# Two-layer graph network on one core: four small operands of VectorE in the second edge pass kept in PSUM in place of SBUF

## The chip, the cores and the metric

The kernel runs on one core of a Trainium2 chip. The metric is the device time of one execution in microseconds (us); the number compared is the median of several executions. Durations of single instructions are in nanoseconds (ns) where marked so. The engines are TensorE (PE; its weight loads are listed as PEld), VectorE (DVE), ScalarE (ACT), GpSimd (POOL) and SyncE (SP).

## The reference, cut to what matters

There are 3125 nodes with 128 features, and 100000 edges (src, dst), sorted by dst in the inputs. Two graph layers follow each other, each with a residual and a layer norm. The change is in the edge work of the second:

```python
def _L1_gnn_ref(X, edge_index, Wq, Wk, Wphi, Wy_w, Wy_b, We):
    src, dst = (edge_index[0], edge_index[1])
    q = (X @ Wq)[src]
    k = (X @ Wk)[dst]
    e = jnp.tanh(q + k)
    scores = e @ Wphi
    scores = scores - jnp.max(scores)
    exp_scores = jnp.exp(scores)
    denom = jax.ops.segment_sum(exp_scores, src, num_segments=N)
    alpha = exp_scores / (denom[src] + 1e-09)
    vy = (X @ Wy_w + Wy_b)[dst]
    ve = e @ We
    msg = alpha[:, None] * (vy + ve)
    out = jax.ops.segment_sum(msg, src, num_segments=N)
    return out
```

## The kernel before, in words

**Stages.** The kernel sorts the edges by src, runs the first layer's edge network and its first edge pass, then the node work between the layers, the second edge pass, and a last node stage. On the profiled execution the second edge pass starts at 1646 us and its last step ends near 2698 us.

**Tiles.** Edges are handled in 196 groups of 512: 128 partitions by 4 (GT). Nodes are handled in 25 blocks of 128 (BN). A step pairs one group with one block that occurs in it. As the edges are sorted by block, there are 220 steps (STEPS, 196 + 25 - 1): mostly a new group, now and then the same group again with the next block. The steps' groups and blocks were worked out on the chip and stand in a plan that the engines read as they go.

**The gathers.** GpSimd does nothing in this pass but fetch the rows of dst (192 numbers, key and value). For every group it issues 4 indirect DMAs (L1575), one for each of the 4 columns, 784 in all. Each takes its 128 row numbers from `rec_all` in SBUF and puts rows of `kv_table` (in DRAM) into one of 8 places (RING1) of `landed_rows`. Before the fourth of a group it waits until the group before has landed, and tells ScalarE (`ready`). From the ninth group on it waits before a group until the step that last used the place is done.

**A step.** All engines keep step through semaphores, each with its instructions in a fixed order, working up to four steps ahead. ScalarE moves the group's landed rows to `row_v` (L1661; tile sum_acc in the profile). VectorE makes `seg_rel`, the node's place in the block (L1723), and the one-hot of it (`hot`, L1726: iota row compared with seg_rel, 128x512, bf16). TensorE transposes the one-hot (L1603), ScalarE copies it (L1690), TensorE takes the queries with it (L1616), VectorE adds them to the keys (`add_queries`, L1740), ScalarE takes tanh (L1671). VectorE multiplies by the attention vector (`score`, L1756, 128x256), sums (L1759), and adds the penalty of edges outside the block and takes the lane's maximum (L1762). ScalarE squares the distance to the block's middle (L1675), VectorE makes the penalty of it (`outside`, L1733). The maximum over the lanes goes through TensorE (L1623), VectorE (`highest`, L1748) and TensorE (L1627) to ScalarE, which makes the exponentials (L1683, 4 a partition) and the factor for the older sums (L1685). VectorE spreads the exponentials over the one-hot (`spread_p`, L1769, 128x512), TensorE forms the messages (L1633), VectorE adds them to the block's sums (`take`, L1780, 128x193).

**What sets the order.** VectorE's order in a step is add_queries two ahead, outside three ahead, hot four ahead, highest one ahead, score two ahead, spread_p one ahead, take. ScalarE's is the row move three ahead, tanh two ahead, the square four ahead, exponentials one ahead, then the copies of query rows (L1667) and transposed one-hot four ahead. Sems `cleared` (GpSimd's three fills) and `cleared_v` (VectorE's fills) hold all three engines back at the start.

**Memory.** The iota row (`iota_n`, 128 columns), attention vector (`phi_b`, 64), penalties (`pen`, 5 steps by 4) and exponentials (`p_e`, 2 by 4) are in SBUF. Of the eight PSUM banks the pass uses 0 to 5; L1740, L1748 and L1780 have one input in PSUM. The instructions that the change touches have both tensor inputs in SBUF:

```python
v.tensor_tensor(onehot_v[...], iota_n..., seg_rel..., ALU.is_equal)     # L1726
v.tensor_tensor(prod[...], row_v[...], phi_b..., ALU.mult)              # L1756
v.tensor_tensor_reduce(sc[...], raw[...], pen[...], ...)                # L1762
v.tensor_tensor(probT_v[...], onehot_v[...], p_e..., ALU.mult)          # L1769
```

Of the kernel before, what the change touches and what calls it, by code (L numbers as in the profile page):

```python
# [5 lines left out]
ALU = mybir.AluOpType  # L6
# [8 lines left out]
AD = 64  # L15
BN = 128
# [5 lines left out]
GT = 4  # L22
# [22 lines left out]
RING = 5  # L45
# [42 lines left out]
def build(nc, i, out):  # L88
    with ExitStack() as ctx:
        def sb(name, shape, dt=F32):  # L90
            return ctx.enter_context(nc.sbuf_tensor(name, shape, dt))
# [21 lines left out]
        iota_n = sb("iota_n", [128, BN])  # L113
# [26 lines left out]
        phi_b = sb("phi_b", [128, AD])  # L140
# [13 lines left out]
        bank = [turn_bank[:, :]] + [twin[n // 2][:, n % 2 * 512:(n % 2 + 1) * 512] for n in range(4)]  # L154
# [3 lines left out]
        def step_of(s, k, ahead=0, unroll=SU):  # L158

            return s + (k + ahead) // unroll, (k + ahead) % unroll  # L160
# [5 lines left out]
        def is_first(n, slots=1):  # L166

            return isinstance(n, int) and n < slots

        def inside(edge, k, ahead, unroll=SU):  # L170


            if edge == "start":
                return k + ahead >= unroll
            return edge is None or k + ahead < edge

        def rounds(eng, body, before, total=STEPS, unroll=SU):

            for k in range(unroll - before, unroll):
                body(-1, k, "start")  # L180
            first = 0
            if total == NB:
                for k in range(unroll):
                    body(0, k, None)
                first = 1
            turns = -(-total // unroll) - 1
            left = total - turns * unroll
            with eng.Fori(first, turns) as s:
                for k in range(unroll):
                    body(s, k, None)  # L190
            for k in range(left):
                body(turns, k, left)
# [796 lines left out]
        with ExitStack() as c2:  # L989
# [14 lines left out]
            onehot_v = onehot[:, :, :].rearrange("p u (j n) -> p u j n", j=GT)  # L1004
# [41 lines left out]
            def within(value, top):  # L1046
                return nc.s_assert_within(value, 0, top, skip_runtime_bounds_check_because="the plan is cut to these bounds")
# [453 lines left out]
        with ExitStack() as c4:  # L1501
            def sb4(name, shape, dt=F32):
                return c4.enter_context(nc.sbuf_tensor(name, shape, dt))

            def sem4(name):
                return c4.enter_context(nc.semaphore(name))
# [12 lines left out]
            onehot_v = onehot[:, :, :].rearrange("p u (j n) -> p u j n", j=GT)  # L1519
# [2 lines left out]
            hotT = sb4("hotT", [BN, 2, GE], BF16)  # L1522
            off = sb4("off_window", [128, 2, GT])
            middle = sb4("middle", [128, 1])
            pen = sb4("pen", [128, RING, GT])
            prod = sb4("prod", [128, GT, AD])
            raw = sb4("raw_score", [128, GT])
            sc = sb4("sc", [128, 2, GT])
# [3 lines left out]
            top_row = sb4("top_row", [1, 128])  # L1532
            top = sb4("top_run", [1, SU])
            neg_top = sb4("neg_top_run", [128, SU])
            p_e = sb4("p_e", [128, 2, GT])

            cleared = sem4("cleared1")
            cleared_v = sem4("cleared1v")
# [9 lines left out]
            prod_done = sem4("prod_done1")  # L1548
# [11 lines left out]
            with nc.Block() as block:  # L1560
# [30 lines left out]
                @block.tensor  # L1591
                def _(pe):
                    pe.sem_inc(stepped, SU)
                    pe.wait_ge(cleared, 3)
                    pe.wait_ge(cleared_v, 5)

                    def turn(s, k):
                        n = s * SU + k
                        if not is_first(n):
                            pe.wait_ge(hotT_done, n)  # L1600
                        pe.wait_ge(hot_done, n + 1)
                        for j in range(GT):
                            last = pe.transpose(bank[1][0:BN, :].bitcast(BF16)[:, j * 128:(j + 1) * 128],  # L1603
                                                onehot_v[:, k % RING, j, :], identb[:, :])
                        last.then_inc(hotT_ps, 1)

                    def queries(s, k):

                        n = s * SU + k
                        pe.wait_ge(q_in, n + 1)  # L1610
                        pe.wait_ge(hotT_done, n + 1)
                        if not is_first(n):
                            pe.wait_ge(sum_done, n)
                        for j in range(GT):
                            for part in range(3):
                                last = pe.matmul(bank[0][:, j * AD:(j + 1) * AD], hotT[:, k % 2, j * 128:(j + 1) * 128],  # L1616
                                                 qb[:, k % RINGQ, part * AD:(part + 1) * AD], start=(part == 0), stop=(part == 2))
                        last.then_inc(query_ps, 1)

                    def turn_max(s, k):  # L1620
                        pe.wait_ge(score_done, s * SU + k + 1)
                        pe.sem_inc(ticks, 1)
                        pe.transpose(bank[2][0:1, 0:128], lane_max[:, k % 2:k % 2 + 1], identf[:, :]).then_inc(maxT_ps, 1)  # L1623

                    def share_top(s, k):
                        pe.wait_ge(top_done, s * SU + k + 1)
                        pe.matmul(bank[3][:, 0:1], ones[0:1, :], top[0:1, k:k + 1], start=True, stop=True).then_inc(top_ps, 1)  # L1627

                    def messages(s, k):
                        pe.wait_ge(spread, s * SU + k + 1)  # L1630
                        pe.wait_ge(summed, s * SU + k + 1)
                        for j in range(GT):
                            last = pe.matmul(bank[4 + k % 2][0:BN, 0:KV + 1], probT_v[:, k % 2, j, :], row_v[:, k % RING, j, AD:RK],  # L1633
                                             start=(j == 0), stop=(j == GT - 1))
                        last.then_inc(stepped, 1)

                    def body(s, k, edge):
                        if inside(edge, k, 1):
                            share_top(*step_of(s, k, 1))
                        if inside(edge, k, 3):  # L1640
                            queries(*step_of(s, k, 3))
                        if inside(edge, k, 4):
                            turn(*step_of(s, k, 4))
                        if inside(edge, k, 2):
                            turn_max(*step_of(s, k, 2))
                        if inside(edge, k, 1):
                            messages(*step_of(s, k, 1))
                    rounds(pe, body, 4)

                @block.scalar  # L1650
                def _(act):
                    act.wait_ge(cleared, 3)
                    act.wait_ge(cleared_v, 5)

                    def move_rows(s, k, at):
                        n = s * SU + k
# [52 lines left out]
                def _(v):  # L1709
# [3 lines left out]
                    v.memset(nil[:, :], 0.0).then_inc(cleared_v, 1)  # L1713
                    v.memset(top[:, :], NONE).then_inc(cleared_v, 1)
                    v.memset(neg_top[:, :], -NONE).then_inc(cleared_v, 1)
                    v.wait_ge(cleared, 3)
                    v.wait_ge(cleared_v, 5)

                    def hot(s, k, g):

                        n = s * SU + k
                        group = rec_all[:, bass.ds(within(g, GROUPS - 1), 1), :].rearrange("p o (j w) -> p (o j) w", w=W2)
                        v.tensor_scalar(seg_rel[:, k % 2, :], group[:, :, 0], base1[:, bass.ds(n, 1)], None,  # L1723
                                        ALU.subtract).then_inc(placed, 1)
                        v.wait_ge(placed, n + 1)
                        v.tensor_tensor(onehot_v[:, k % RING, :, :], iota_n[:, :].unsqueeze(1).to_broadcast([128, GT, BN]),  # L1726
                                        seg_rel[:, k % 2, :].unsqueeze(2).to_broadcast([128, GT, BN]),
                                        ALU.is_equal).then_inc(hot_done, 1)

# [22 lines left out]
                    def score(s, k):  # L1752

                        n = s * SU + k
                        v.wait_ge(tanh_done, n + 1)
                        v.tensor_tensor(prod[:, :, :], row_v[:, k % RING, :, KV:KV + AD],  # L1756
                                        phi_b[:, :].unsqueeze(1).to_broadcast([128, GT, AD]), ALU.mult).then_inc(prod_done, 1)
                        v.wait_ge(prod_done, n + 1)
                        v.tensor_reduce(raw[:, :], prod[:, :, :], AX.X, ALU.add).then_inc(raw_done, 1)  # L1759
                        v.wait_ge(raw_done, n + 1)  # L1760
                        v.sem_inc(ticks, 1)
                        v.tensor_tensor_reduce(sc[:, k % 2, :], raw[:, :], pen[:, k % RING, :], 1.0, floor[:, 0:1],  # L1762
                                               ALU.add, ALU.max, lane_max[:, k % 2:k % 2 + 1]).then_inc(score_done, 1)
# [194 lines left out]
```

## Time and profile before

| | |
|---|---|
| median of 3 runs | 2787.11 us (2782.03 to 2795.92) |
| the profiled execution, its own time | 2772.86 us |
| its span, first to last instruction | 2771.2 us |
| mean granted TensorE clock in it | 0.898 of full |
| TensorE / weight loads busy | 78% / 52% of the span |
| VectorE, ScalarE, GpSimd busy | 66%, 55%, 61% |

The profile is of one execution. "Busy" counts the time in which an engine has an instruction under way; "idle before" is the time an engine stood still just ahead of a group of instructions, with what ended it ("issue": nothing that the profile shows). A line with a q behind the engine's name is its sequencer. The shares are a mean over stages with different limits. The profiled execution took 14.3 us less than the median of the runs.

### The profile page before, as it was taken

What the parts mean: (1) busy time and instruction counts of PE and PEld (TensorE: products, weight loads), DVE (VectorE), ACT (ScalarE), POOL (GpSimd) and SP (SyncE); (2) the same over time, 40 slices, a digit from 0 to 9 for tenths busy, and PEclk for the clock granted to TensorE, in tenths of its full rate; (3) what the DMA queues carried; (4) which work ended last, traced back from release to release, by engine and by line L of the source; (5) the groups of instructions that cost most, each with busy time, mean ns of one, the idle gap of its engine ahead of it and who ended that gap; (6) DMA issues with size and microseconds to landing.
All of it is one profiled execution on the core that took longest, in us unless ns stands there. A gap on an engine that the chain in (4) does not pass through costs nothing. (4 is left out here: it accounts for less than half of the span.)

```text
span 2771.2 us, 64649 instructions
## 1 busy us (share of the span) xinstructions
PE 2167.7 (78%) x16604; PEld 1454.2 (52%) x16604; DVE 1815.4 (66%) x6215; ACT 1528.7 (55%) x4445; POOL 1687.2 (61%) x1772
## 2 busy tenths in 40 slices
PE   6799999996888888888888376776777777777773
PEld 4333333334666666666667345555555555555552
DVE  8965464105666666766666637777778777777764
ACT  2466766774555555555554115555555555555541
POOL 1377777765555565556552017777777777777750
PEclk9999999997999999999999658889888889888985
DMA  9244444544444444444443012222222222222220
GB/s 97 72 137 130 134 134 145 143 114 133 152 153 154 156 149 150 155 149 151 156 149 104 5 43 76 74 75 74 74 76 77 75 73 74 77 77 75 76 53 24
DMA packets 211670, 290.63 MB, mean 105 GB/s; under 512 B 87104, under 2 KB 136149, under 8 KB 211568
## 3 DMA queue, kind: packets, MB, share of 16 engines
q0 software_dynamic: 76160, 172.95, 23.0%
q1 hardware_dynamic: 135408, 116.54, 14.1%
q8 instruction: 38, 0.62, 0.1%
q14 instruction: 64, 0.52, 0.1%
HBM read 183.24 MB, written 28.70 MB: 76 GB/s over the span
## 5 line engine op out<-in xcount | busy, mean ns | idle before, releaser
L1575 POOL DMA_INDIRECT sum_acc<-kv_table,rec_all x784 | 790.0, 1008 | 239.2 <-issue 229.9
L1079 POOL DMA_INDIRECT area_b<-h_table,src_g x448 | 454.6, 1015 | 339.9 <-issue 184.7
L514 POOL DMA_INDIRECT early<-h_table,src_g x336 | 331.2, 986 | 222.0 <-ACT sum_acc L729 142.0
L729 ACT ACTIVATE sum_acc<-twin,bias 128x1024 f32<-128x1024 f32 x294 | 317.9, 1117 | 155.1 <-PE twin L599 151.3
L1661 ACT COPY sum_acc<-sum_acc 128x768 f32 x220 | 183.4, 834 | 378.0 <-POOLq L1581 290.4
L1176 ACT COPY y_sb<-bank 128x512 f32<-128x512 f32 x293 | 171.5, 585 | 329.4 <-PE bank L1140 327.7
L1149 PE MATMUL bank<-hs,y_sb 128*128 128x129 f32 x2344 | 323.6, 282 | 0.7 <-ACT y_sb L1172 0.6
L599 PE MATMUL twin<-area_b,wc 64*128 64x512 f32 x1176 | 313.5, 634 | 10.9 <-ACT sum_acc L729 10.9
L1140 PE MATMUL bank<-identf,hs 128*128 128x128 f32 x1172 | 196.2, 292 | 138.9 <-DMA hs<-area_b 137.2
L1149 PEld LDWEIGHTS bank<-hs,y_sb 128*128 128x128 f32 x2344 | 296.8, 198 | 5.1 <-issue 3.8
L1267 DVE SCALAR_TENSOR_TENSOR sum_acc<-sum_acc,shrink,bank 128x129 f32 x293 | 102.2, 349 | 277.0 <-ACT m_old L1193 172.6
L1633 PE MATMUL bank<-sum_acc,probT 128*128 128x193 f32 x880 | 222.5, 408 | 27.0 <-DVE probT L1769 24.6
L1140 PEld LDWEIGHTS bank<-identf,hs 128*128 128x128 f32 x1172 | 128.5, 146 | 205.9 <-issue 205.9
L1633 PE MATMUL twin<-sum_acc,probT 128*128 128x193 f32 x880 | 214.3, 397 | 26.9 <-DVE probT L1769 24.9
L1633 PEld LDWEIGHTS bank<-sum_acc,probT 128*128 128x128 f32 x880 | 181.7, 234 | 53.1 <-DVE probT L1769 52.1
L1633 PEld LDWEIGHTS twin<-sum_acc,probT 128*128 128x128 f32 x880 | 174.5, 226 | 52.9 <-DVE probT L1769 51.5
L1756 DVE TENSOR_TENSOR prod<-sum_acc,phi_b 128x256 f32<-128x256 f32 x220 | 93.7, 426 | 152.8 <-ACT sum_acc L1671 151.5
L1623 PE MATMUL twin<-identf,lane_max 128*1 128x128 f32 x220 | 63.1, 287 | 163.8 <-DVE lane_max L1762 163.7
L599 PEld LDWEIGHTS twin<-area_b,wc 64*128 64x128 f32 x1176 | 95.7, 186 | 155.7 <-issue 78.9
L1769 DVE TENSOR_TENSOR probT<-onehot,p_e 128x512 f32<-128x512 bf16 x220 | 152.0, 691 | 11.9 <-ACT p_e L1683 11.8
L1726 DVE TENSOR_TENSOR onehot<-iota_n,seg_rel 128x512 bf16<-128x512 f32 x220 | 153.4, 697 | 7.6
L1235 DVE TENSOR_TENSOR y_sb<-onehot,w_g 128x384 f32<-128x384 bf16 x293 | 157.1, 536 | 0.0
(311 smaller groups left out, 4540.1 us busy)
## 6 DMA issues: line engine op xcount, KB each, us to landing
hs<-area_b SPq DMA_DIRECT2D x293, 258.0 KB, 2.4
area_b<-in_edge_attr SPq DMA_DIRECT2D x97, 256.0 KB, 2.9
rows_table<-early POOLq DMA_DIRECT2D x84, 258.0 KB, 3.0
area_b<-rows_table POOLq DMA_DIRECT2D x84, 258.0 KB
sum_acc<-kv_table,rec_all POOLq DMA_INDIRECT x784
area_b<-h_table,src_g POOLq DMA_INDIRECT x448
early<-h_table,src_g POOLq DMA_INDIRECT x336
kv_table<-sum_acc SPq DMA_DIRECT2D x25, 96.0 KB, 1.6
```

The costliest lines, as they stand in the source:

```text
L514: pool.indirect_dma_start(out=early[:, g % RINGE, j, 0:D], out_offset=None, in_=h_table, in_offset=bass.IndirectOffsetOnAxis(ap=src_g[:, e ...
L599: pe.matmul(twin[p % 2][:, half * GE:(half + 1) * GE], wc[half * DE:(half + 1) * DE, m * D:(m + 1) * D], eaT[half * DE:(half + 1) * DE, o ...
L729: act.activation(hid_words[:, first:first + 2 * GE], twin[p % 2][:, :], ACT.Relu, bias=bias1[:, m:m + 1]).then_inc(hid_sb, 1)
L1079: pool.indirect_dma_start(out=landed_rows[:, k * GT + j, 0:D], out_offset=None, in_=h_table, in_offset=bass.IndirectOffsetOnAxis(ap=src_g[ ...
L1140: last = pe.transpose(bank[0][:, j * 128:(j + 1) * 128], hs[:, k % SH, j, 0:D], identf[:, :])
L1149: last = pe.matmul(bank[5 + k % 3][:, 0:D + 1], both[:, k % 4, j, :], hs[:, k % SH, j, :], start=(j == 0), stop=(j == GT - 1))
L1176: act.copy(hsT[:, k % 2, :], bank[0][:, :]).then_inc(hsT_done, 1)
L1235: v.tensor_tensor(both[:, k % 4, :, WN:].rearrange("p j (m n) -> p j m n", m=M), onehot_v[:, k % SH, :, :].unsqueeze(2).to_broadcast([128, ...
L1575: pool.indirect_dma_start(out=landed_rows[:, g % RING1 * GT + j, :], out_offset=None, in_=kv_table, in_offset=bass.IndirectOffsetOnAxis(ap ...
L1633: last = pe.matmul(bank[4 + k % 2][0:BN, 0:KV + 1], probT_v[:, k % 2, j, :], row_v[:, k % RING, j, AD:RK], start=(j == 0), stop=(j == GT - 1))
L1661: act.copy(row_v[:, k % RING, :, 0:KV], landed_rows[:, bass.ds(within(at, (RING1 - 1) * GT), GT), :]).then_inc(moved, 1)
L1726: v.tensor_tensor(onehot_v[:, k % RING, :, :], iota_n[:, :].unsqueeze(1).to_broadcast([128, GT, BN]), seg_rel[:, k % 2, :].unsqueeze(2).to ...
```

## The change

The iota row and the attention vector are copied once, at the start of the pass, to PSUM bank 6. The penalties are written by VectorE to bank 6, the exponentials by ScalarE to bank 7. The four instructions above read them there. `cleared_v` counts two more.

```diff
-            pen = sb4("pen", [128, RING, GT])
...
-            p_e = sb4("p_e", [128, 2, GT])
+            iota_ps = bank[6][:, 0:BN]
+            phi_ps = bank[6][:, BN:BN + AD]
+            pen = bank[6][:, 256:256 + RING * GT].rearrange("p (u j) -> p u j", u=RING)
+            p_e = bank[7][:, 0:2 * GT].rearrange("p (q j) -> p q j", q=2)
...
                     pe.wait_ge(cleared, 3)
-                    pe.wait_ge(cleared_v, 5)
+                    pe.wait_ge(cleared_v, 7)
...
                     act.wait_ge(cleared, 3)
-                    act.wait_ge(cleared_v, 5)
+                    act.wait_ge(cleared_v, 7)
...
                     v.memset(neg_top[:, :], -NONE).then_inc(cleared_v, 1)
+                    v.tensor_copy(iota_ps, iota_n[:, :]).then_inc(cleared_v, 1)
+                    v.tensor_copy(phi_ps, phi_b[:, :]).then_inc(cleared_v, 1)
                     v.wait_ge(cleared, 3)
-                    v.wait_ge(cleared_v, 5)
+                    v.wait_ge(cleared_v, 7)
...
-                        v.tensor_tensor(onehot_v[:, k % RING, :, :], iota_n[:, :].unsqueeze(1).to_broadcast([128, GT, BN]),
+                        v.tensor_tensor(onehot_v[:, k % RING, :, :], iota_ps.unsqueeze(1).to_broadcast([128, GT, BN]),
                                         seg_rel[:, k % 2, :].unsqueeze(2).to_broadcast([128, GT, BN]),
                                         ALU.is_equal).then_inc(hot_done, 1)
...
                         v.tensor_tensor(prod[:, :, :], row_v[:, k % RING, :, KV:KV + AD],
-                                        phi_b[:, :].unsqueeze(1).to_broadcast([128, GT, AD]), ALU.mult).then_inc(prod_done, 1)
+                                        phi_ps.unsqueeze(1).to_broadcast([128, GT, AD]), ALU.mult).then_inc(prod_done, 1)
```

L1733, L1762, L1683 and L1769 keep their text; their `pen` and `p_e` are now in PSUM.

## Rows read from the trace of the kernel before

**Rows 1.** The page, busy us (share of the span) and instructions

```profile
PE 2167.7 (78%) x16604; PEld 1454.2 (52%) x16604; DVE 1815.4 (66%) x6215; ACT 1528.7 (55%) x4445; POOL 1687.2 (61%) x1772
```

**Rows 2.** Busy time of each engine from 1651 to 2680 us

```profile
sum 1029.00, PE 736.14 PEld 577.57 DVE 788.54 ACT 594.72 POOL 789.93; mean PE 184.03 PEld 144.39 DVE 197.14 ACT 148.68 POOL 197.48
```

**Rows 3.** GpSimd's gathers: page group (busy, mean ns, idle); line (ns min/median/max), waits

```profile
L1575 POOL DMA_INDIRECT sum_acc<-kv_table,rec_all x784 | 790.0, 1008 | 239.2 <-issue 229.9
...
L1575 POOL DMA_INDIRECT sum_acc<-kv_table,rec_all x784: 940/946/1467, 1651.0 to 2679.1; - x196
...
  DMA sum_acc<-kv_table,rec_all: 6.4, 21
```

**Rows 4.** The page's groups, ScalarE's move of landed rows

```profile
L1661 ACT COPY sum_acc<-sum_acc 128x768 f32 x220 | 183.4, 834 | 378.0 <-POOLq L1581 290.4
```

**Rows 5.** Timeline (start, duration in us), VectorE's L1780 in two successive steps

```profile
2216.20 0.41 DVE L1780 SCALAR_TENSOR_TENSOR area_b<-area_b,shrink_,bank 128x193 f32 x1
...
2219.99 0.41 DVE L1780 SCALAR_TENSOR_TENSOR area_b<-area_b,shrink_,twin 128x193 f32 x1
```

**Rows 6.** Groups of GpSimd from 2200 to 2300 us

```profile
L1575 POOL DMA_INDIRECT sum_acc<-kv_table,rec_all x74 | 78.1, 1056 | 22.9 <-issue 21.6 <-DMA sum_acc<-kv_table,rec_all 0.9 <-PE twin L1633 0.3
```

**Rows 7.** Timeline, three of the 31 long gathers and VectorE's instruction beside each

```profile
2209.33 0.41 DVE L1756 TENSOR_TENSOR prod<-sum_acc,phi_b 128x256 f32<-128x256 f32 x1
2209.36 1.21 POOL L1575 DMA_INDIRECT sum_acc<-kv_table,rec_all  x1 [0.63 <-issue]
...
2234.13 0.69 DVE L1769 TENSOR_TENSOR probT<-onehot,p_e 128x512 f32<-128x512 bf16 x1
...
2234.46 1.18 POOL L1575 DMA_INDIRECT sum_acc<-kv_table,rec_all  x1 [0.30 <-issue]
...
2299.47 0.69 DVE L1726 TENSOR_TENSOR onehot<-iota_n,seg_rel 128x512 bf16<-128x512 f32 x1
...
2299.56 1.43 POOL L1575 DMA_INDIRECT sum_acc<-kv_table,rec_all  x1 [0.30 <-issue]
```

**Rows 8.** Timeline, gathers that begin while L1740 or L1780 runs

```profile
2273.95 0.42 DVE L1740 TENSOR_TENSOR sum_acc<-bank,sum_acc 128x256 f32<-128x256 f32 x1
2274.01 0.95 POOL L1575 DMA_INDIRECT sum_acc<-kv_table,rec_all  x1 [0.30 <-issue]
...
2302.47 0.41 DVE L1780 SCALAR_TENSOR_TENSOR area_b<-area_b,shrink_,bank 128x193 f32 x1
2302.54 0.95 POOL L1575 DMA_INDIRECT sum_acc<-kv_table,rec_all  x1 [0.30 <-issue]
```

**Rows 9.** Groups of VectorE and ScalarE by shape (busy us, mean ns)

```profile
L1726 DVE TENSOR_TENSOR onehot<-iota_n,seg_rel 128x512 bf16<-128x512 f32 x220 | 153.4, 697 | 7.6
L1769 DVE TENSOR_TENSOR probT<-onehot,p_e 128x512 f32<-128x512 bf16 x220 | 152.0, 691 | 11.9 <-ACT p_e L1683 11.8
L782 DVE TENSOR_TENSOR area_b<-area_b 128x512 f32<-128x512 f32 x146 | 100.0, 685 | 0.0
L1756 DVE TENSOR_TENSOR prod<-sum_acc,phi_b 128x256 f32<-128x256 f32 x220 | 93.7, 426 | 152.8 <-ACT sum_acc L1671 151.5 <-issue 0.4
L1740 DVE TENSOR_TENSOR sum_acc<-bank,sum_acc 128x256 f32<-128x256 f32 x220 | 93.4, 424 | 27.4 <-issue 13.9 <-ACT sum_acc L1661 5.0
...
L1733 DVE TENSOR_SCALAR pen<-off_window 128x4 f32<-128x4 f32 x220 | 36.5, 166 | 0.0
...
L782 DVE TENSOR_TENSOR area_b<-area_b,bank 128x512 f32<-128x512 f32 x7 | 4.8, 680 | 0.0
...
L1685 ACT ACTIVATE shrink_<-neg_top_run 128x1 f32<-128x1 f32 x220 | 61.3, 279 | 0.0
...
L1680 ACT ACTIVATE neg_top_run<-twin 128x1 f32<-128x1 f32 x220 | 35.7, 162 | 60.2 <-PE twin L1627 58.0
```

**Rows 10.** Timeline of the pass's start, GpSimd's large fill and VectorE's last

```profile
1646.69 4.11 POOL L1568 MEMSET area_b<- 128x4825 f32 x1
...
1647.01 0.07 DVE L1715 MEMSET neg_top_run<- 128x10 f32 x1
```

## Prediction

> **What bounds the kernel now.** The change touches one stage, the second edge pass, so I read in this order: the page's busy shares, the busy times of that stage, GpSimd's transfers, the waits, and last the timeline around single transfers. Over the whole span no engine is full [rows 1]. In the pass, from GpSimd's first row gather at 1651.0 us to the end of its last at 2680.05 us, a stretch of 1029 us, VectorE is busy 789 us and GpSimd 790 us [rows 2], a tie that tells nothing. The gaps decide. GpSimd's 784 gathers leave only 239.2 us idle in front of them, 0.305 us each; 229.9 us of that is GpSimd's own issue time, and the 21 gaps put down to a landed transfer average 6.4/21 = 0.305 us, no longer than the others [rows 3]. 790.0 + 239.2 = 1029.2 us: GpSimd goes from one gather to the next without a pause and is the whole stretch. The other side waits for it: ScalarE's move of the landed rows, once a step, waits 290.4 us in total for GpSimd [rows 4]. VectorE can do a step in 3.79 us when rows are there [rows 5], where a step now gets 1029/220 = 4.68 us. So the pass lasts as long as GpSimd's 784 gathers, and a VectorE instruction made faster or slower costs nothing by itself. What counts is what the change does to a gather.
>
> **What lengthens a gather.** A gather has a median of 946 ns, but a mean of 1008 and a maximum of 1467 [rows 3]. 784 x (1008 - 946) = 48.6 us is the excess. In the stretch from 2200 to 2300 us the mean is 1056 ns over 74 [rows 6]. I went through these 74 beside VectorE's timeline: 31 are over 960 ns, and each of the 31 began while L1726, L1769 or L1756 was running, and ended some 0.82 us after that instruction did. The first of them, one between, and the last: L1756 ends at 2209.74, the gather at 2210.57; L1769 at 2234.82, the gather at 2235.64; L1726 at 2300.16, the gather at 2300.99 [rows 7]. What these three have in common is two tensor inputs in SBUF. Where L1740 or L1780 runs across a gather's beginning the gather takes 0.95 us [rows 8]; these are as long, but one of their two tensors is in PSUM. So GpSimd, at the start of a gather, seems to need something that a VectorE instruction with two SBUF inputs holds until its end, and one with a single SBUF input leaves free. The change makes exactly these three (and the short L1762) instructions with one SBUF input.
>
> A page speaks against this reading. The Trainium skill, "SBUF — State Buffer", section "Who interferes with whom", infers that a two-input tensor operation takes only the read half of the ports VectorE shares with GpSimd, while descriptor generation needs the write half, so that such an operation would not stall it; by that there is nothing to gain. The timeline here shows such stalls, up to 1467 - 946 = 521 ns, so the sum goes by the rows.
>
> **The change part by part.**
> - L1726 (iota to PSUM), L1769 (exponentials to PSUM), L1756 (attention vector to PSUM): each loses its second SBUF input. GpSimd: all 784 gathers at 946 ns, so -48.6 us, all of it on the path. The order of operands differs (the PSUM one is first in L1726, second in the others); L1740 has it first, L1780 second, and neither stalls a gather [rows 8], so I take the whole.
> - The length of these instructions. Same operation, same 128x512 shape: L782 with both inputs in SBUF 685 ns, with one in PSUM 680; at 128x256, both in SBUF 426 (L1756), one in PSUM 424 (L1740) [rows 9]. So the price of a PSUM input is -5 to 0 ns, and I take 0. What no row shows is a PSUM operand read with repetition, as iota, vector and exponentials are here; the low end is 0, the high end, a read at half rate, is priced under the rivals.
> - The penalty (L1733) is written to PSUM and L1762 reads it there. No row has VectorE writing PSUM. L1733 takes 166 ns [rows 9]; I bound it by that much either way and take 0. It lies under GpSimd's pace; without that cover it is at most 220 x 0.17 = 37 us.
> - ScalarE writes the exponentials (L1683) to PSUM. No row has that either. The nearest pair is one-column work from PSUM, 162 ns (L1680), against one from SBUF, 279 ns (L1685) [rows 9]: a memory moved on the read side is worth 117 ns. Bounds +/-0.12 us a step, value 0; hidden by the same cover, at most 26 us if it is gone. ScalarE's row move (L1661) still waits behind GpSimd.
> - Two copies at the start, and a wait for 7 in place of 5 on three engines. 128 and 64 columns, by L1740's 424 ns for 256 under 0.8 us for both. VectorE is through its fills at 1647.1 us and then waits for GpSimd's 4.11 us fill, which ends at 1650.8 [rows 10]: 3.7 us of cover. TensorE and ScalarE wait for the same fill. Cost 0; at most 0.8 us if GpSimd's fill were gone. No DMA and no queue is moved, and GpSimd's program is unchanged.
>
> Sum: the stretch falls from 1029.2 to 784 x (0.946 + 0.305) = 980.8 us, -48.6 us (the three decimals round). The profiled execution goes from 2772.9 to about 2724 us. It was faster than all runs shown, whose median, 2787.1, is 14.3 us above it; I keep that distance and forecast 2738.5 us, 1.7% less. What is late next is still GpSimd, at 4 x 1.251 = 5.0 us a group; 220 steps over 196 groups then have 980.8/220 = 4.46 us each, against 3.79 in a free step. A landing will not be late: none delays a gather beyond the ordinary 0.305 us now [rows 3], and 3 gathers still lie between a group's last gather and the wait for it.
>
> **The rivals.**
> - A, slower: repeated reads from PSUM run at half rate. From 128x256 to 128x512 an SBUF instruction grows by (697 - 426)/256 = 1.06 ns an element [rows 9]; again as much for 512, 512 and 256 elements is +1.36 us a step, 3.79 + 1.36 = 5.15 us x 220 = 1133 us against 1029: +104 us, 2891 us. It decides as soon as the addition passes 4.68 - 3.79 = 0.89 us a step; from 0.67 us on it begins to eat the gain. For it: no row shows such a read. Against: all PSUM inputs in the rows run at SBUF's rate. The Trainium skill, "VectorE: DVE Perf Modes", section "The TRN2 errata", gives a VectorE access to PSUM 62 cycles more than to SBUF, an estimate of 65 ns each; the pairs above do not show it, and it would only move the point nearer. Chance 5%.
> - B, no change: GpSimd's stall is bound to VectorE's length or output, not to its second SBUF input, and stays. For it: L1726 and L1769 are the longest instructions and write the most. Against: L1756, as short as L1740, stalls too, and L1740 does not. This is also the outcome in which the change does not do what it says. 2787 us, chance 7%.
> - C, a part: L1726, which keeps its repeated SBUF operand beside PSUM, goes on stalling. Of the 74 x (1056 - 946) ns = 8.1 us excess in the stretch [rows 6], 5.1 us lie in the 15 gathers that L1726 held, the last gather of [rows 7] among them, so the gain is 48.6 x 3.0/8.1 = 18 us: 2769 us. Against it: L1740 has the same placing, PSUM first and SBUF second. Chance 8%.
>
> **How the numbers follow.** The forecast has 80%. Its own range: runs of before spread by -5 to +9 us about their median, and the excess, read from one execution, may be 40 to 60 us; 2722 to 2756 us. To hold 8 in 10 with the rivals I reach to C: 2722 to 2770. A measurement of this kernel can tell about 0.5%, 14 us, from no change. Faster by over that: the forecast and most of C, 0.86. Within: B and the rest of C, 0.09. Slower: A, 0.05.
>
> **What would show it.** Right: the gather's mean at 946 to 955 ns with a maximum near its median, the gap still 0.305 us, the stretch near 981 us; no gather ending 0.82 us after a VectorE instruction; the one-hot, product and spread instructions within 20 ns of their 697, 426 and 691 ns; everything before 1646 us and after the pass as before. Wrong: a mean of 1008 again (B), about 985 with long gathers at the one-hot alone (C), or long VectorE instructions and GpSimd waiting for steps, gaps over 0.305 us (A).

## The result, and the profile after

The changed kernel takes 2724.9 us in the median (2722.85 to 2725.70, 4 runs), the kernel before 2788.61 us (2782.03 to 2795.92, 4 runs). The ratio is 0.977, with a 95% interval of 0.9744 to 0.9795: faster by 63.7 us, where 48.6 us were forecast. The profiled spans differ by 2771.2 - 2724.1 = 47.1 us, nearly the forecast. The missing 16 us and the spread of the runs, 14 us before and 3 us after, belong together, as the experiments make likely. One execution of x_iota below (3563.93 us) and one of the kernel before beside it (2817.20 us) fell into a slower state at a lower granted clock and are left out of the medians and ratios.

The page of the changed kernel (engine, busy us, share of the span, instructions) first, then its groups of the gathers and of ScalarE's row move (busy, mean ns | idle before them, releaser); they answer to [rows 1, 3, 4]:

```profile
PE 2136.3 (78%) x16604; PEld 1429.2 (52%) x16604; DVE 1810.1 (66%) x6217; ACT 1531.8 (56%) x4445; POOL 1639.0 (60%) x1772
...
L1577 POOL DMA_INDIRECT sum_acc<-kv_table,rec_all x784 | 741.3, 946 | 240.0 <-issue 235.9
...
L1663 ACT COPY sum_acc<-sum_acc 128x768 f32 x220 | 183.4, 834 | 306.7 <-POOLq L1583 189.6
```

GpSimd lost 48.1 us of busy time in the whole kernel (1687.2 to 1639.0), and 790.0 - 741.3 = 48.7 us of it in the 784 gathers of this pass. The idle time before them is what it was (239.2, now 240.0 us). VectorE's busy time over the kernel fell by 5 us only. The rows' wait of ScalarE for GpSimd fell from 290.4 to 189.6 us and is still large: GpSimd remains the bound.

The line view of the gathers (ns min/median/max, first and last start in us, then what ended the idle time: us, times):

```profile
L1577 POOL DMA_INDIRECT sum_acc<-kv_table,rec_all x784: 941/946/959, 1652.6 to 2632.8; - x196
...
  issue: 235.9, 770
  PE bank L1635: 2.7, 9
  PE twin L1635: 0.9, 3
  DMA sum_acc<-kv_table,rec_all: 0.3, 1
```

The median is the old one, 946 ns; the maximum is 959 where it was 1467 [rows 3]. Not one gather is held any more: "held" is said here of a gather of over 960 ns that ends some 0.82 us after a VectorE instruction does. From the first to the end of the last the stretch is 981 us where it was 1029.

VectorE's and ScalarE's groups by shape, in the pass, which answer to [rows 9]; "bank" is now the iota row, the exponentials, the attention vector or the penalties:

```profile
L1730 DVE TENSOR_TENSOR onehot<-bank,seg_rel 128x512 bf16<-128x512 f32 x220 | 152.2, 692 | 7.5
L1773 DVE TENSOR_TENSOR probT<-onehot,bank 128x512 f32<-128x512 bf16 x220 | 150.5, 684 | 15.7 <-ACT bank L1685 13.4 <-issue 2.3
L1760 DVE TENSOR_TENSOR prod<-sum_acc,bank 128x256 f32<-128x256 f32 x220 | 91.7, 417 | 105.2 <-ACT sum_acc L1673 104.7
L1766 DVE CUSTOM_DVE_ANT_0 sc<-raw_score,bank,floor 128x4 f32<-128x4 f32 x220 | 48.1, 219 | 41.6 <-DVE raw_score L1763 39.3 <-issue 2.3
L1737 DVE TENSOR_SCALAR bank<-off_window 128x4 f32<-128x4 f32 x220 | 34.0, 154 | 0.0
L1685 ACT ACTIVATE bank<-sc,neg_top_run 128x4 f32<-128x4 f32 x220 | 58.8, 267 | 0.0
```

The three long ones went from 697, 691 and 426 to 692, 684 and 417 ns in the mean (medians 693, 687 and 425 to 692, 683 and 421), the write of the penalty from 166 to 154. A repeated read from PSUM cost no time here. The start of the pass, in the timeline (start, us), which answers to [rows 10]:

```profile
1648.23 4.11 POOL L1570 MEMSET area_b<- 128x4825 f32 x1
...
1648.55 0.27 DVE L1718 COPY bank<-iota_n 128x128 f32<-128x128 f32 x1
...
1648.74 0.20 DVE L1719 COPY bank<-phi_b 128x64 f32<-128x64 f32 x1
```

Both copies end at 1648.94, 3.4 us before GpSimd's fill does.

### The profile page after: what moved, and what is told of

Same layout as the page of the kernel before. It is cut to its first block and busy times, and to the rows that moved or that the text cites. A ratio compares the mean times of both kernels' runs of the same rounds, so it can differ in the third digit from the quotient of the medians.

```text
span 2724.1 us, 64651 instructions
## 1 busy us (share of the span) xinstructions
PE 2136.3 (78%) x16604; PEld 1429.2 (52%) x16604; DVE 1810.1 (66%) x6217; ACT 1531.8 (56%) x4445; POOL 1639.0 (60%) x1772
## 5 line engine op out<-in xcount | busy, mean ns | idle before, releaser
L1577 POOL DMA_INDIRECT sum_acc<-kv_table,rec_all x784 | 741.3, 946 | 240.0 <-issue 235.9
L1663 ACT COPY sum_acc<-sum_acc 128x768 f32 x220 | 183.4, 834 | 306.7 <-POOLq L1583 189.6
L1635 PE MATMUL twin<-sum_acc,probT 128*128 128x193 f32 x880 | 204.7, 384 | 28.7 <-DVE probT L1773 28.4
L1635 PE MATMUL bank<-sum_acc,probT 128*128 128x193 f32 x880 | 205.7, 385 | 25.5 <-DVE probT L1773 24.1
L1635 PEld LDWEIGHTS bank<-sum_acc,probT 128*128 128x128 f32 x880 | 167.8, 219 | 50.9 <-DVE probT L1773 50.5
L1635 PEld LDWEIGHTS twin<-sum_acc,probT 128*128 128x128 f32 x880 | 166.0, 217 | 53.5 <-DVE probT L1773 53.5
L1760 DVE TENSOR_TENSOR prod<-sum_acc,bank 128x256 f32<-128x256 f32 x220 | 91.7, 417 | 105.2 <-ACT sum_acc L1673 104.7
L1773 DVE TENSOR_TENSOR probT<-onehot,bank 128x512 f32<-128x512 bf16 x220 | 150.5, 684 | 15.7 <-ACT bank L1685 13.4
L1730 DVE TENSOR_TENSOR onehot<-bank,seg_rel 128x512 bf16<-128x512 f32 x220 | 152.2, 692 | 7.5
```

The lines of the kernel that those rows point to most:

```text
L1577: pool.indirect_dma_start(out=landed_rows[:, g % RING1 * GT + j, :], out_offset=None, in_=kv_table, in_offset=bass.IndirectOffsetOnAxis(ap ...
L1663: act.copy(row_v[:, k % RING, :, 0:KV], landed_rows[:, bass.ds(within(at, (RING1 - 1) * GT), GT), :]).then_inc(moved, 1)
L1730: v.tensor_tensor(onehot_v[:, k % RING, :, :], iota_ps.unsqueeze(1).to_broadcast([128, GT, BN]), seg_rel[:, k % 2, :].unsqueeze(2).to_broa ...
```

## The experiments

The theory: a gather that starts while a VectorE instruction with two tensor inputs in SBUF is running is held until that instruction ends; GpSimd is the bound of the pass, so each us of hold is a us of the kernel. The main rivals: length or output of the VectorE instruction holds the gather, whatever memory it reads; or the gain came on another way, from shorter work of VectorE or ScalarE.

For each profile I went through the gathers of over 960 ns as in the prediction and set each down to the instruction that ended some 0.82 us before it. The table has these counts, with the us that they hold, beside the mean of all 784 gathers and the median of the executions (us). Chips and batches differ; the ratio to the kernel before on the same chip stands with each experiment.

| kernel | median | mean gather, ns | by the one-hot | by the spread (L1769) | by the product (L1756) |
|---|---|---|---|---|---|
| before, profile of the forecast | 2788.6 | 1008 | 113, 31.0 us | 45, 10.9 us | 36, 6.7 us |
| before_again | 2783.4 | 1018 | 130, 37.8 us | 60, 13.0 us | 41, 6.1 us |
| x_phi | 2806.6 | 1051 | 148, 51.2 us | 93, 31.6 us | in PSUM: 0 |
| x_pe | 2750.6 | 985 | 100, 24.4 us | in PSUM: 0 | 31, 6.4 us |
| x_iota | 2738.9 | 964 | in PSUM: 0 | 51, 10.9 us | 23, 3.7 us |
| x_iota_pe | 2725.6 | 949 | 0 | 0 | 33, 2.9 us |
| changed kernel | 2724.9 | 946 | 0 | 0 | 0 |

In these seven profiles the span goes from 2724.0 to 2805.0 us, but the span less the busy time of the 784 gathers is always between 1978.3 and 1982.7 us. So the gain is in the gathers, and the rival that it came on another way falls.

The traces also give the edges of a hold. In the first profile of before, 175 gathers begin at least 0.05 us after the start of one of the three instructions and at least 0.15 us before its end, and all 175 are held (969 ns or more); in before_again it is 221 of 221, in x_phi 230 of 230. A gather that begins less than 0.13 us before the instruction's end is not held by it: 0.13 us is what is left of its 946 ns when the 0.82 us after the hold are taken off. And where the gather begins within 44 ns of the instruction's start, it runs at its usual length and VectorE waits instead (115 of the 117 that begin 0 to 44 ns behind it, in these three profiles; two were held):

```profile
2200.26 0.49 DVE L1756 TENSOR_TENSOR prod<-sum_acc,phi_b 128x256 f32<-128x256 f32 x1 [0.83 <-ACT sum_acc L1671]
2200.30 0.95 POOL L1575 DMA_INDIRECT sum_acc<-kv_table,rec_all  x1 [0.31 <-PE twin L1633]
```

Here L1756 takes 0.49 us where its median is 0.425. So the one that comes first delays the other. VectorE's share of it is small: the three instructions are longer 64 times in the first profile of before, by up to 75 ns and 2.7 us together; in the changed kernel none is.

**before_again.** The kernel before, without an edit, for a second profile.

> The kernel before, unchanged, for a second profile of it. The change gained 63.7 us in the medians but 47.1 us in the two profiled spans, and the one profiled execution of before was its fastest. If the whole gain is GpSimd's held gathers, an execution of before that takes some 2787 us shows a mean gather above 1008 ns: 1008 + (2787 - 2773)/0.784 = about 1026 ns, and nothing else longer. If the 15 us lie elsewhere, the mean gather is 1008 ns again and another stage is longer.

The median was 2783.41 us, ratio 0.998 (0.9948 to 1.0013). The profiled execution took 2781.3 us with a span of 2779.7. Its groups of the gathers:

```profile
L1575 POOL DMA_INDIRECT sum_acc<-kv_table,rec_all x784 | 798.2, 1018 | 239.4 <-issue 227.9 <-DMA sum_acc<-kv_table,rec_all 7.6 <-PE bank L1633 2.1
```

The span is 8.5 us longer than that of the first profile, the gathers' busy time 8.2 us. So the kernel before differs from run to run (2773.7 to 2797.5 us in ten runs of this label) by how many gathers happen to be held, and two executions agree with that one for one. The expectation's formula, 1008 + (2781.3 - 2772.9)/0.784, gives 1019 ns, and 1018 was measured. That settles the 16 us for the part that two profiles can: the first profile was of an execution with few held gathers. None was taken of an execution as long as the median, so the rest of the 16 us is likely and not shown.

**x_iota, x_pe, x_phi.** One operand each goes to PSUM, in the kernel before (left out here: the counts of `cleared_v` that go with it).

```diff
 x_iota
+            iota_ps = bank[6][:, 0:BN]
+                    v.tensor_copy(iota_ps, iota_n[:, :]).then_inc(cleared_v, 1)
-                        ... iota_n[:, :].unsqueeze(1).to_broadcast([128, GT, BN]),
+                        ... iota_ps.unsqueeze(1).to_broadcast([128, GT, BN]),
 x_pe
-            p_e = sb4("p_e", [128, 2, GT])
+            p_e = bank[7][:, 0:2 * GT].rearrange("p (q j) -> p q j", q=2)
 x_phi
+            phi_ps = bank[6][:, BN:BN + AD]
+                    v.tensor_copy(phi_ps, phi_b[:, :]).then_inc(cleared_v, 1)
-                        ... phi_b[:, :].unsqueeze(1).to_broadcast([128, GT, AD]), ALU.mult)
+                        ... phi_ps.unsqueeze(1).to_broadcast([128, GT, AD]), ALU.mult)
```

> Only the iota row is moved to PSUM; L1769, L1756 and L1762 keep two SBUF inputs. Theory (a gather is held by a VectorE instruction with two SBUF inputs that runs across its start): the gathers held by the one-hot are gone, the others stay; of the 48.6 us excess in the first profile, 63% lay at the one-hot in the stretch looked at, so 30 us of gain or somewhat less, since the freed gathers start at other times and may now meet L1769 or L1756 more often; mean gather 960 to 975 ns. Rival (VectorE's length or output holds the gather): no gain, mean 1008 ns or more. Long gathers end some 0.82 us after an L1769 or L1756, none after a one-hot.

> Only the exponentials are in PSUM (written there by ScalarE, read by L1769). Theory: the gathers held by L1769 are gone; by its share in the stretch, 1.8 of 8.1 us, about 11 us of gain if the other instructions hold no more gathers than before. Rival (length or output): 0 us. Rival (the exponentials' shorter way from ScalarE to VectorE is what gains): a gain with the mean gather at 1008 ns.

> Only the attention vector is in PSUM (L1756). Theory: the gathers held by L1756 are gone; 1.2 of 8.1 us in the stretch, about 7 us of gain if the one-hot and L1769 hold no more than before. Rival (length or output): 0 us. If the three single gains do not add up to 64 us, the held gathers depend on each other through their starting times, which the share of each line in the three profiles will show.

x_iota: 2738.90 us (3 executions), ratio 0.9833 (0.9781 to 0.9885), 48 us of gain by the medians of 2787.16 and 2738.90, where 30 were expected. x_pe: 2750.62 us, 0.9867 (0.9827 to 0.9907), 37 us, where 11 were expected. x_phi: 2806.59 us, 1.0067 (1.0039 to 1.0095), 19 us slower, where 7 us of gain were expected. The gathers of the three:

```profile
L1576 POOL DMA_INDIRECT sum_acc<-kv_table,rec_all x784 | 756.1, 964 | 240.0 <-issue 231.6 <-DMA sum_acc<-kv_table,rec_all 6.7 <-PE bank L1634 1.5
```

```profile
L1575 POOL DMA_INDIRECT sum_acc<-kv_table,rec_all x784 | 772.2, 985 | 239.1 <-issue 230.4 <-DMA sum_acc<-kv_table,rec_all 4.3 <-PE twin L1633 2.1
```

```profile
L1576 POOL DMA_INDIRECT sum_acc<-kv_table,rec_all x784 | 824.2, 1051 | 239.0 <-issue 223.6 <-DMA sum_acc<-kv_table,rec_all 12.5 <-PE bank L1634 1.5
```

In each kernel the instruction whose operand moved holds no gather any more, and the two others go on: the kind of hold is as the theory says, and the rival of length or output falls. The sizes of the gains were missed in all three, x_phi's in its sign. They do not add either: 48 + 37 - 19 = 66 us is near the measured 64 only by accident, since x_phi's part is a loss: the holds of one instruction depend on when the others have let the gathers start. The timeline of x_phi (start, us) shows the link:

```profile
2316.09 0.69 DVE L1771 TENSOR_TENSOR probT<-onehot,p_e 128x512 f32<-128x512 bf16 x1
...
2316.39 1.21 POOL L1576 DMA_INDIRECT sum_acc<-kv_table,rec_all  x1 [0.30 <-issue]
...
2317.80 0.69 DVE L1728 TENSOR_TENSOR onehot<-iota_n,seg_rel 128x512 bf16<-128x512 f32 x1
2317.90 1.41 POOL L1576 DMA_INDIRECT sum_acc<-kv_table,rec_all  x1 [0.30 <-issue]
```

A gather held by the spread ends 0.82 us after it, and the next begins 0.30 us later, at 2317.90: 1.12 us after the spread's end. VectorE's next one-hot begins 1.02 us after the spread's end, at 2317.80, as it does within 0.03 us in about half of the steps (110 of 216 in this profile). So the next gather starts 0.10 us into the one-hot and is held almost for its whole length (1.41 us). Such a pair, a gather held by the spread and the next by the one-hot, occurs 24 times in the first profile of before, 38 times in before_again and 67 times in x_phi. So holds by the spread drag holds by the one-hot with them: with the spread's gone (x_pe) the one-hot held 24.4 us, where it held 31.0 and 37.8 in the two profiles of before, and with more of them (x_phi) 51.2. That is a part of x_pe's surplus over 11 us. The other part, and most of x_iota's over 30, is likely that the expectations were scaled to the first profile, which has fewer holds than the median execution: profile against profile the spans differ by 20.7 us for x_pe and by 33.9 us for x_iota. Why the spread meets more gathers once the product no longer holds any (93 against 45 and 60) was not taken apart further: the start of the gathers shifts against the step, and more is not shown.

**x_iota_pe.** The iota row and the exponentials are moved together; the attention vector and the penalties stay in SBUF (left out here: the counts of `cleared_v`).

```diff
 changed kernel
-            phi_ps = bank[6][:, BN:BN + AD]
-                    v.tensor_copy(phi_ps, phi_b[:, :]).then_inc(cleared_v, 1)
-                        ... phi_ps.unsqueeze(1).to_broadcast([128, GT, AD]), ALU.mult)
+                        ... phi_b[:, :].unsqueeze(1).to_broadcast([128, GT, AD]), ALU.mult)
-            pen = bank[6][:, 256:256 + RING * GT].rearrange("p (u j) -> p u j", u=RING)
+            pen = sb4("pen", [128, RING, GT])
```

> Iota row and exponentials in PSUM; attention vector and penalties stay in SBUF, so L1756 is the one long instruction with two SBUF inputs. The attention vector alone made the kernel slower, and the question is whether moving it is worth anything once the others are moved. Theory: L1756 holds 25 to 50 gathers for 0.15 us each, mean gather 951 to 955 ns, 4 to 8 us slower than the changed kernel. Rival (moving the attention vector is harmful in itself): faster than the changed kernel.

2725.55 us, ratio 0.9792 (0.9773 to 0.981). The changed kernel on the same chip took 2721.48 us, 0.9784 (0.9768 to 0.9801). 4.1 us by the medians, at the low end of what was expected, with intervals that overlap; 2.9 us of held gathers at L1756 in the profile and nothing at L1762. So the attention vector's move, harmful alone, is worth some 3 us beside the two others by the trace, and the penalties' nothing that can be seen.

**after_again.** The changed kernel, without an edit, as the base on this chip.

> The changed kernel once more, beside the next three on one chip, as the base for differences of a few us. Theory: 2723 to 2727 us with executions within 4 us of each other, where the kernel before spreads over 20 us and more: with no gather held, nothing is left that differs from run to run.

2721.48 us, five executions from 2720.20 to 2725.22, while nine of before on the same chip went from 2774.61 to 2786.92. The median is 1.5 us under the expected range and the spread, 5.0 us, a little over the 4 expected; before spread over 12 us here. That no hold is left does not make the runs equal: y_start, without a hold in its profile, went from 2720.84 to 2729.87 us. What moves them is open.

**y_two, y_one.** One more VectorE instruction a step, that nobody reads; the two kernels differ in the memory of one constant.

```diff
+            spare = sb4("spare", [128, GT, 64])
...
                                         ALU.is_equal).then_inc(hot_done, 1)
+                        v.tensor_tensor(spare[:, :, :], iota_n[:, 0:64].unsqueeze(1).to_broadcast([128, GT, 64]),
+                                        ones[:, 0:64].unsqueeze(1).to_broadcast([128, GT, 64]),
+                                        ALU.mult)
 in y_one:      iota_ps[:, 0:64] in place of iota_n[:, 0:64]
```

> The changed kernel with one more VectorE instruction a step behind the one-hot: a 128x256 product of two constants, both in SBUF, that nobody reads. Theory: some 0.42 us more for VectorE in each step, under the cover of GpSimd's pace, and gathers that start in it are held until its end: mean gather 955 to 970 ns with single ones up to 1.25 us, 8 to 20 us slower than the changed kernel. Rival (only length or output count): as y_one, whatever that does.

> The same as y_two, with the first constant read from PSUM instead of SBUF; same size, same place, same output. Theory: no gather is held, mean 946 ns, and 3.77 + 0.42 = 4.2 us a free step is still less than the 4.46 us that GpSimd gives: within 3 us of the changed kernel. Rival (length or output): held gathers and the same loss as y_two.

y_two: 2728.21 us, ratio 0.9792 (0.9763 to 0.982). y_one: 2726.44 us, 0.9789 (0.9759 to 0.9818). In time the two can't be told apart, and y_two lost less than the 8 us expected. The changed kernel was not run beside them; y_one is 1.5 us over its first median and 5.0 over that of after_again, where within 3 was expected, so this is open. The traces can tell them apart. First the extra instruction and the gathers of y_two, with one held gather of its timeline:

```profile
L1734 DVE TENSOR_TENSOR spare<-iota_n,ones 128x256 f32<-128x256 f32 x220 | 92.0, 418 | 0.0
...
L1578 POOL DMA_INDIRECT sum_acc<-kv_table,rec_all x784: 943/949/1191, 1649.3 to 2636.8; - x196
...
1709.66 0.42 DVE L1734 TENSOR_TENSOR spare<-iota_n,ones 128x256 f32<-128x256 f32 x1
1709.71 1.19 POOL L1578 DMA_INDIRECT sum_acc<-kv_table,rec_all  x1 [0.30 <-issue]
```

Then the same two views of y_one:

```profile
L1734 DVE TENSOR_TENSOR spare<-bank,ones 128x256 f32<-128x256 f32 x220 | 91.2, 415 | 0.0
...
L1578 POOL DMA_INDIRECT sum_acc<-kv_table,rec_all x784: 945/949/964, 1650.6 to 2632.7; - x196
```

The same size, place and output: with both inputs in SBUF it holds 38 gathers for 5.9 us together and the maximum is 1191 ns; with one in PSUM it holds none and the maximum is 964, 951 where it meets this instruction. Gathers that begin at least 0.05 us after its start and 0.15 us before its end are 37 in y_two, all held, and 30 in y_one, none held. From the first gather to the end of the last it is 988.6 us in y_two and 983.1 in y_one, 5.6 us more, close to the 5.9 of the holds. This is the cleanest evidence for the theory. It also shows that 0.42 us more of VectorE in each of 220 steps, 91 us, cost nothing that can be measured: y_swap, below, is without the instruction and took 2727.07 us on the same chip.

**y_swap.** The two inputs of the one-hot in the other order.

```diff
-  onehot_v[...], iota_ps.unsqueeze(1).to_broadcast([128, GT, BN]), seg_rel[...].unsqueeze(2).to_broadcast([128, GT, BN]),
+  onehot_v[...], seg_rel[...].unsqueeze(2).to_broadcast([128, GT, BN]), iota_ps.unsqueeze(1).to_broadcast([128, GT, BN]),
```

> The changed kernel with the operands of the one-hot in the other order: the repeated SBUF operand first, the PSUM row second. Theory (the number of SBUF inputs counts, not which place they have): mean gather 946 ns, same time as the changed kernel within 3 us. Rival (the second place is what counts): also 946 ns here, since PSUM has the second place; a difference would say that the first place counts.

2727.07 us, ratio 0.9791 (0.9762 to 0.9819), mean gather 945 ns. One SBUF input holds nothing in either place.

**y_start, y_start_again.** Two of GpSimd's three fills at the start of the pass go to VectorE.

```diff
-                    pool.memset(acc_st, 0.0).then_inc(cleared, 1)
-                    pool.memset(top_st, NONE).then_inc(cleared, 1)
...
+                    v.memset(acc_st, 0.0).then_inc(cleared, 1)
+                    v.memset(top_st, NONE).then_inc(cleared, 1)
                     v.memset(floor[:, :], -BIG).then_inc(cleared_v, 1)
```

> The changed kernel with two of GpSimd's three fills at the pass's start (4.11 us for the 128x4825 one, 0.12 us for the other) given to VectorE, which waits there. The output stays the same. If GpSimd's work is the whole stretch, its first gather starts 4 us earlier and the kernel ends about 4 us earlier, 2721 us, since VectorE's fill of the same size is over before the first group has landed. If another engine set the end, no difference.

> The kernel with two of GpSimd's fills given to VectorE once more, now beside the changed kernel itself. In the first run's profile the first gather starts 0.8 us after the pass begins, against 4.4 us in the changed kernel. Theory: 3 to 4 us below after_again. Rival (only chance between batches): no difference.

y_start took 2722.07 us (0.9778, 0.9752 to 0.9804) beside y_one's 2726.44 and y_swap's 2727.07; y_start_again took 2720.54 us (0.9774, 0.9757 to 0.979) beside 2721.48 of the changed kernel. The second comparison is the fair one; 3 to 4 us were expected, and the 0.9 us measured are less than the spread of either. The timeline of y_start_again:

```profile
1649.65 0.13 POOL L1569 MEMSET sum_acc<- 128x20 f32 x1 [164.29 <-SPq L1562]
1650.45 0.95 POOL L1575 DMA_INDIRECT sum_acc<-kv_table,rec_all  x1 [0.67 <-issue]
```

The first gather begins 0.80 us after the pass does; in the changed kernel it is 1652.56 - 1648.18 = 4.38 us. These 3.6 us are gained on GpSimd and the stretch of gathers that follows is as long as before (981.7 us). But the pass itself began at 1643.8 us in the profile of after_again and at 1649.6 in this one, with the same program up to there. The stages ahead differ by more than what is gained. Whether the 3.6 us reach the end of the kernel is likely by the trace and not shown by the times.

**y_slow.** Two more 128x512 VectorE instructions a step, each with one input in PSUM.

```diff
+            spare = sb4("spare", [128, 2, GT, 128])
...
+                        v.tensor_tensor(spare[:, 0, :, :], iota_ps[:, 0:128].unsqueeze(1).to_broadcast([128, GT, 128]),
+                                        ones[:, 0:128].unsqueeze(1).to_broadcast([128, GT, 128]),
+                                        ALU.mult)
 and the same once more into spare[:, 1, :, :]
```

> The changed kernel with two more 128x512 VectorE instructions a step behind the one-hot, each with one input in PSUM: 2 x 0.69 = 1.38 us a step. A free step then takes 3.77 + 1.38 = 5.15 us, more than the 4.46 us that GpSimd gives. Theory: the steps become the bound, 220 x 5.15 = 1133 us for the pass in place of 981, some 2875 us in all; gathers still 946 ns, with GpSimd waiting for steps in between. Rival (the cover is larger, since part of a step's VectorE time overlaps): under 2800 us.

One execution, 2852.84 us, 131 us over the 2721.48 of the changed kernel on this chip; expected were some 150. The gathers in the line view of y_slow:

```profile
L1578 POOL DMA_INDIRECT sum_acc<-kv_table,rec_all x784: 940/946/962, 1650.6 to 2739.5; - x196
...
  issue: 232.7, 731
  PE bank L1636: 58.2, 23
  PE twin L1636: 55.3, 21
```

No gather is held, though VectorE is busier than ever, and GpSimd now waits 58.2 + 55.3 = 113.5 us for finished steps. From 1650.6 to 2740.4 us the 220 steps get 4.95 us each, where 5.15 were expected: of the 2 x 680 ns added, 4.95 - 3.77 = 1.18 us lengthen a free step (3.77 us is the step from 2159.93 to 2163.70 us in the profile of the changed kernel). The expectation added durations, but in the timeline the two instructions and the one behind them start 0.60 us apart, each before the one ahead of it has ended: 2 x 0.60 = 1.20 us. So GpSimd's cover is real and ends about where it was put: 0.42 us a step cost nothing that can be measured, 1.36 us did.

## Why the prediction was right, and where it was off

- **The bound.** Right. The gathers, at 946 + 306 ns, are 981 us of the pass after the change as computed (980.8), and shortening them shortened the kernel; VectorE's extra 91 us in y_one did not lengthen it measurably, and y_slow shows where that stops.
- **What lengthens a gather.** Right, and now shown by the pair y_two and y_one. Two edges were not seen: a gather that begins in the first 44 ns of the instruction goes first and delays VectorE, and only the first 0.13 us of a gather can be held. The Trainium skill, "SBUF — State Buffer", section "Who interferes with whom", also says plainly that a VectorE instruction with two SBUF inputs contends with a GpSimd instruction that reads SBUF; the trace agrees (38 held gathers against none). Its inference in brackets, that descriptor generation needs the write half of the ports only, would leave the gathers of this kernel unheld, and they are held: the maximum fell from 1467 to 959 ns. It may still hold for most of a gather: in y_two the extra instruction begins 123 times later than 0.25 us into a gather, and none of these gathers takes over 957 ns. That the open 0.13 us are the reading of the row numbers from SBUF would fit both, and is argued, not shown.
- **All 784 gathers at 946 ns.** Right to the nanosecond, and 48.7 us between the two profiles where 48.6 was forecast. The size is that close because both numbers are of the same execution of before; against before_again it is 56.9 us.
- **The price of PSUM inputs, 0.** Right: -5, -7 and -9 ns for the three, -4 for L1762. The Trainium skill, "VectorE: DVE Perf Modes", section "The TRN2 errata", has 62 cycles more for PSUM, some 65 ns as an estimate; no row here shows it, and the twin instructions of y_two and y_one measure 418 and 415 ns. Part of the gain in the means is the waiting for gathers that is gone; by the medians it is 1, 4 and 4 ns.
- **Writes to PSUM, 0 with bounds.** Inside the bounds and gains both: -12 ns for VectorE's, -30 ns for ScalarE's (297 to 267). Hidden. Of the 12 ns only 3 are in the median (158 to 155); the rest are single instructions of up to 375 ns, told below.
- **The start.** Right: the copies take 0.27 and 0.20 us and end 3.4 us before GpSimd's fill does.
- **The absolute time, 2738.5 us against 2724.9 measured.** Off by 13.6 us, inside the range. The step that failed is the sentence "I keep that distance": the 14.3 us by which the median lay above the profiled execution were taken for something that stays. By all that the profiles show they were held gathers too: a second profile of before, 8.5 us longer, had 8.2 us more of them, and with none held the profiled execution (2725.7) is no longer apart from the median (2724.9). The excess of the gathers should have been scaled to the median run: 48.6 + 14.3 = 62.9 us, where 63.7 were measured. My bound on it, 40 to 60 us, was a guess where the spread of the runs shown could have given it.
- **Rival C's sharing by lines.** It would have misled: it took 30 us for the one-hot and 18 for the rest, while x_iota gained 48, x_pe 37, and x_phi lost 19. Shares of a wait read from one profile are not what taking each away brings, when a wait moves the start of the next.
- **Rivals A and B.** Both fell: repeated reads from PSUM run at 684 to 692 ns for 512 elements, and the holds are gone.

## What to carry to other kernels

When an engine goes from one instruction to the next without a pause, look at its mean against its median: the excess may be another engine's doing, and the timeline tells which instruction's end the long ones follow. A VectorE instruction with two tensor inputs in SBUF, beside a GpSimd that gathers, is such a neighbour; one input in PSUM removes the hold at no price seen here. That it pays was shown here where GpSimd is the bound, and only there. Move all such instructions or measure: moving only the product's made this kernel slower.

## What the runs showed that was not expected

- Taking away the holds of the shortest instruction alone cost 19 us (1.0067, 1.0039 to 1.0095), through 93 holds by the spread where there were 45 and 60, and pairs of holds: 0.82 us from the end of the spread to the end of the gather, 0.30 us to the next gather, while the next one-hot starts 1.02 us after the spread's end.
- The kernel before had a spread of 12 to 28 us from run to run in its four batches, and two profiles put their difference on these meetings; the changed kernel has 3 to 5 us.
- GpSimd holds VectorE too, near the end of a gather. L1733, one input and the output in SBUF, took up to 375 ns in the first profile of before (median 158), and the six of over 250 ns ended 3 to 10 ns before a gather did. With its output in PSUM it never took over 166 ns. L1723, which stays in SBUF, took up to 464 ns before and 467 after. None of this is on the path here.
- ScalarE's exponentials are 30 ns shorter when written to PSUM (267 against 297 ns).
